# Three one-hot comparisons of 1,024 values in place of one of 3,072 in the bucket stage of a graph layer kernel

## The reference

```
gate = sigmoid(log u - log(1-u) + log_alpha)           # log_alpha from both ends' features
mask = clip(gate * (ZETA - GAMMA) + GAMMA, 0, 1)        # one weight per edge
d    = clip((segment_sum(mask, row) + EPS_DEG) ** -0.5, 0, 10)
out  = segment_sum(mask * d[row] * d[col] * x[col], row)
```

## Time and profile before

| | |
|---|---|
| median of three runs | 6101.76 us |
| profiled execution | 6092.52 us |
| its span | 6090.7 us |
| VectorE busy | 5120.7 us, 84% |
| TensorE matmuls busy | 4148.6 us, 68% |
| ScalarE busy | 2501.2 us, 41% |
| GpSimd busy | 1389.0 us, 23% |
| bucket stage of layer 0, first DMA issue to last one-hot | 3338.7 to 3867.5 us |
| bucket stage of layer 1, the same | 5548.4 to 6082.0 us |

### The profile page before, as it was taken

The page is one execution under the profiler, slowest core; times in us unless marked ns, Lnnn a source line. Parts: engine busy times, 40 slices in busy tenths (PEclk is TensorE's granted clock), DMA queues, the critical chain, the costliest instruction groups (busy, mean ns, idle before and its releaser), DMA issues. The chain is left out here.

```text
span 6090.7 us, 161651 instructions
## 1 busy us (share of the span) xinstructions
PE 4148.6 (68%) x56330; PEld 3706.6 (61%) x56330; DVE 5120.7 (84%) x10244; ACT 2501.2 (41%) x5126; POOL 1389.0 (23%) x1562
## 2 busy tenths in 40 slices
PE   3777777776597888835554666888888355554666
PEld 2666666665456888825443666558888344444565
DVE  8999999999446999989998777229999799997776
ACT  2666656564134555425554000245555155551000
POOL 0000000000002333300000888303333100004887
PEclk9777777776555555566776999755555577777999
DMA  3000000000136777569997898336767499997888
GB/s 71 0 0 0 0 0 0 0 0 1 14 12 215 232 233 232 192 218 331 329 330 280 298 310 299 113 101 231 234 230 232 143 317 330 330 330 267 310 313 282
DMA packets 428686, 1120.74 MB, mean 184 GB/s; under 512 B 206962, under 2 KB 212707, under 8 KB 428023
## 3 DMA queue, kind: packets, MB, share of 16 engines
q1 hardware_dynamic: 316700, 549.97, 29.3%
q0 software_dynamic: 65856, 316.89, 15.1%
q10 hardware_dynamic: 46036, 252.74, 10.9%
HBM read 873.65 MB, written 279.36 MB: 189 GB/s over the span
## 5 line engine op out<-in xcount | busy, mean ns | idle before, releaser
L1610 PE MATMUL psG<-y_window,area 128*128 128x64 bf16 x14976 | 675.1, 218 | 774.4 <-DVE area L1256 620.4
L1610 PEld LDWEIGHTS psG<-y_window,area 128*128 128x128 bf16 x14976 | 631.3, 115 | 818.4 <-issue 504.5
L586 POOL DMA_INDIRECT work<-msg_d,widx x396 | 584.0, 1475 | 1643.4 <-issue 1605.7
L642 ACT ACTIVATE work<-iota,work 128x149 bf16<-128x149 f32 x2496 | 789.0, 406 | 0.0
L1429 PE MATMUL psG<-area,work 128*128 128x112 bf16 x2496 | 550.8, 390 | 338.0 <-DVE area L978 338.0
L1622 PE MATMUL psG<-work,edge 128*128 128x192 bf16 x4752 | 483.2, 263 | 306.9 <-DVE edge L1290 306.9
L1622 PEld LDWEIGHTS psG<-work,edge 128*128 128x128 bf16 x4752 | 448.0, 147 | 341.5 <-DVE edge L1290 259.9
L1429 PEld LDWEIGHTS psG<-area,work 128*128 128x128 bf16 x2496 | 357.4, 148 | 486.3 <-issue 341.3
L1422 PE MATMUL psG<-work,merge 128*128 128x148 bf16 x4992 | 546.3, 294 | 68.2 <-ACT work L642 68.2
L1422 PEld LDWEIGHTS psG<-work,merge 128*128 128x128 bf16 x4992 | 529.6, 132 | 90.9 <-issue 66.6
L816 ACT ACTIVATE work<-merge 128x1024 bf16<-128x1024 f32 x312 | 330.1, 1058 | 549.4 <-DVE merge L1266 549.4
(11 more groups left out here) (268 smaller groups left out, 8385.7 us busy)
## 6 DMA issues: line engine op xcount, KB each, us to landing
msg_d<-work ACTq DMA_DIRECT2D x312, 776.0 KB, 4.6
area<-rlo_d SPq DMA_DIRECT2D x312, 512.0 KB, 4.4
merge<-crel_d SPq DMA_DIRECT2D x312, 512.0 KB, 5.0
area<-crelp_d SPq DMA_DIRECT2D x312, 512.0 KB, 5.7
y_window<-y_d SPq DMA_DIRECT2D x312, 48.0 KB, 3.6
y_d<-cur SPq DMA_DIRECT2D x7, 1008.0 KB, 3.8
y_d<-work SPq DMA_DIRECT2D x7, 1008.0 KB, 4.8
work<-msg_d,widx POOLq DMA_INDIRECT x396, 6.2
```

Source lines behind the costliest of these rows:

```text
L586: pool.indirect_dma_start(out=windows[par][:, rows.start:rows.stop, :].rearrange("p s w -> p (s w)"), out_offset=None, in_=msg_d, in_offse ...
L642: ins = act.activation(below[:, h, k, :], iota_all[:, :], ACT.Sign, bias=keyf[:, bass.ds(t * CT + k, 1)], scale=-1.0)
L1610: ins = pe.matmul(psG[:, 2 * h + k // CH, k % CH * D:(k % CH + 1) * D], col_one_hots[:, h, k * P:(k + 1) * P], y_window[:, h, m * D:(m + 1 ...
```

## The change

The one-hots of a bucket are made group by group. Each of the three comparisons writes 1,024 values per partition (8 rows by 128 nodes) and counts `q_hots_ready` by one, so that a bucket counts three. TensorE waits before its matmuls 0, 8 and 16 for the count of the group that they use, and no longer for all three groups before the first. The count of matmuls, their order, the DMAs, the buffers and the values stay as they are.

```
-                    dve.tensor_tensor(q_one_hots[s], iota_rows.unsqueeze(1).to_broadcast([P, WG, P, WIN]),
-                                      ids[:, s, :].rearrange("p (g s) -> p g s", g=WG).unsqueeze(2).to_broadcast([P, WG, P, WIN]), ALU.is_equal).then_inc(q_hots_ready, 1)
+                    for g in range(WG):
+                        dve.tensor_tensor(q_one_hots[s][:, g, :, :], iota_rows,
+                                          ids[:, s, g * WIN:(g + 1) * WIN].unsqueeze(1).to_broadcast([P, P, WIN]), ALU.is_equal).then_inc(q_hots_ready, 1)
...
-                        pe.wait_ge(q_hots_ready, n + 1)
                         for r in range(WG * WIN):
+                            if r % WIN == 0:
+                                pe.wait_ge(q_hots_ready, n * WG + r // WIN + 1)
                             ins = pe.matmul(psG[:, slot_, 0:MW], q_one_hots[slot_][:, r // WIN, :, r % WIN], windows[slot_][:, r, 0:MW],
                                             start=r == 0, stop=r == WG * WIN - 1)
```

## The result

The changed kernel took 5891.02 us (median of four runs, 5883.25 to 5891.75) against 6100.96 us for the kernel before (median of four): a ratio of 0.9652, 95% interval 0.9637 to 0.9668. The profiled execution took 5890.85 us, 201.7 us less than the one before; its span is 5889.1 us. The forecast was 5985 us with a range down to 5925: the sign and the mechanism were right, but little more than half of the gain was forecast. The time is that of the rival with VectorE as the bound at 2.9 us a bucket, and half of its reason holds as well, as the experiments show.

The account below looks back on a forecast made before the run. GpSimd's DMA issuing, held by VectorE's comparisons, was taken to bound the bucket stages at 3.585 us a bucket; transfers at 3.2 would follow, saving 113 us over 294 buckets plus 2 us: 5985 us, range 5925 to 6065.

Parts of the forecast that it names:

- the rival with VectorE as the bound at 2.9 us a bucket: Bucket stages: transfers are no bound, VectorE sets 2.9 us a bucket; 5899 us, chance 0.12.
- The stage is paced by GpSimd's issuing: Bucket stages before the change: two GpSimd DMA issues with gaps take 3.56 us a bucket, matching the measured pace.
- An issue that starts while a comparison runs stands still until its end and then needs 0.87 us: GpSimd's DMA issues in the bucket stages: held by VectorE's comparison, losing 0.48 us an issue, 282 us over 294 buckets.
- Does the lock open between two comparisons?: Step claiming, from the mask stage, that GpSimd gets in between back-to-back comparisons, so thirds hold an issue only one third.
- The slower rival: Bucket stages: issues are not let in between thirds, each bucket loses 0.15 us; 6146 us, chance 0.06.
- Part 1: VectorE's added fixed cost per bucket: three comparisons take 1.91 us against 1.76, +0.15 us, ends 0 and 0.30.
- Part 2: VectorE's floor per bucket with data there: 2.67 us before, 2.82 with thirds, 2.9 with small gaps.
- Part 3: GpSimd's issuing per bucket after the change: two issues of 1.10 us with 0.30 us gaps, 2.8 us.
- Part 4: Transfers become the longest: 3.07 us a bucket at 349 GB/s, 3.25 at 330, 3.2 taken.
- The sum: (3.585 - 3.2) x 294 = 113 us plus 2 us at the ends, 115 us off 6092.5; median forecast 5985 us.
- Part 5: TensorE starts 1.07 us earlier, worth nothing inside the bucket stage, 2 us over the last buckets of both layers.
- GpSimd waits more than 0.3 us for TensorE would say it has run ahead: Sign in the bucket stage: GpSimd has reached the buffers' limit and the transfers are the bound.

Follow-up runs that it names:

- e5: The kernel before with every indirect DMA fetching half its rows, as many issues; 6088.76 us, ratio 0.9986.
- e9: The kernel before, one comparison of 3,072 values, with `ids` in float32 in PSUM, so one comparison input in SBUF; 6312.37 us.
- e10: The kernel before, one comparison of 3,072 values, with `ids` in float32 in SBUF, so both comparison inputs in SBUF; 6537.95 us.
- e4: The changed kernel with every indirect DMA fetching half its rows, as many issues; 5882.83 us.
- e8: The kernel before, making only 128 of a bucket's 3,072 one-hot values, which all matmuls use; 5890.78 us.
- e1: The changed kernel, still three comparisons, but TensorE waits for all three before its first matmul; 5894.16 us.
- e3: The changed kernel with only the first group's comparison made, its one-hots used by all 24 matmuls; 5891.75 us.
- e7: The changed kernel with the previous bucket's sum moved behind the first third and its scaling behind the second; 5890.24 us.

## Why the prediction was right or wrong

- "The stage is paced by GpSimd's issuing": right. e5 shows it from the other side: half the bytes, the same 3.57 us.
- "An issue that starts while a comparison runs stands still until its end and then needs 0.87 us": right. In the kernel before 290 of the 302 issues that started within a comparison ended 0.85 to 0.90 us after its end; the other 12 started in its first 0.04 us and took 1.00 us. e9 with e10 give the cause.
- "Does the lock open between two comparisons?": it does. In the changed kernel's timeline an issue ends 0.87 us after the first third, while the second and the third run. The slower rival falls with it. The Trainium skill (SBUF — State Buffer, Who interferes with whom) infers that `tensor_tensor` spares descriptor generation, since that needs the write interface alone. For an indirect DMA, whose offsets lie in SBUF, the runs show otherwise: 3.96 us in e10 against 0.99 us in e9. The same section's rule on two SBUF inputs agrees with both.
- Part 1, +0.15 us for thirds: the row of three is 1.90 us in the timeline against 1.91. Right.
- Part 2, VectorE's floor of 2.82 to 2.9 us: 2.84 in e4 and in the changed kernel, layer 0. Right.
- Part 3, issues of 1.10 us and 2.8 us a bucket: (210.9 + 117.5) / 294 = 1.117 us, 2.84 us, and none over 1.51 us. Right.
- **Part 4 is the step that failed**: "At 349 a bucket takes 3.07 us, at 330 3.25. I take 3.2". The sum's term for the transfers was mis-sized: their limit is 380 GB/s and 2.81 us a bucket in layer 0 (e8), not 3.2. I read a limit from the best 10 us and from a stage of another kind of transfer. Even those 10 us were short of work: their DMA share is 0.95, where e8 at its limit has 1.00. The trace had said so at a finer grain: the DMA view of 20 us of the kernel before, in 40 slices of 0.5 us (first row the share in tenths), has slices of over 400 GB/s beside others at a quarter of it.

```profile
DMA  9994296899951967999659379895969999999995
GB/s 410 410 354 180 106 199 161 310 385 422 397 199 75 137 87 273 385 447 410 242 213 174 99 273 410 348 248 149 236 248 410 422 422 422 342 422 422 422 404 211
```

  The longest run of full slices there is at 404 to 422 but for one of 342, 410 in the mean, above what the queue holds over a stage (380), so these overstate as the 10 us windows understate; the truth lay between. With the measured 2.89 us in place of 3.2 the sum gives (3.585 - 2.89) x 294 + 2 = 206 us, and the profiled executions differ by 202. With the transfers at 2.81 us, VectorE's 2.82 to 2.9 us of part 2 becomes the longest term in layer 0. (The sum's own last step gives 5986.5 and is written as 5985; nothing hangs on it.)
- Part 5, TensorE's early start worth 2 us: e1 puts it at 3 to 9 us. Small, as forecast; the runs do not tell it more finely.
- The rival "the transfers are no bound at all and VectorE is" has the measured time and half of the cause. VectorE does set the pace in layer 0, and the sign listed for it, VectorE without idle time at 2.9 us, was seen: 0.6 us of waits for data in 332 us. But the transfers are a bound right behind it: in e3 VectorE had 1.0 us less to do and the time stayed, and in e7 the shorter cycle turned into waits for data. That the two limits lie so close is chance of this kernel. The rival should have had more than 0.12, since nothing in the rows excluded rates above 349.
- "GpSimd waits more than 0.3 us for TensorE would say it has run ahead": seen in layer 1, where the waits for buffers reach 1.4 us (`POOL area L586 <- PE psG L1624: 8.3, 17, 1.4` in the table of waits). Layer 1 is 0.07 us a bucket slower than layer 0. In e8, with neither VectorE nor the issues in the way, it is as well (2.85 and 2.92 us a bucket between the first and the last `ids`), so the difference lies with the transfers or with what else they share. The output stored during that stage is a candidate that I did not try; it has the size: from 5480 to 5850 us the changed kernel's DMA view counts 137.39 MB of indirect transfers and 4.10 MB in another queue, which leaves the indirect ones 371 GB/s against 379 in layer 0, 2% or 0.06 us a bucket.

## What to carry to other kernels

When one engine's instruction holds another's, count how many of the held ones fit between two of the holders, and not the mean delay: here one comparison of 1.76 us let through one issue where a bucket needs two, and cutting it in two or three removed 196 or 210 us for 0.07 us of VectorE's time a cut. Cut no further than that, as the eight pieces show. And when a bound is taken away, do not read the next resource's limit from the stage in which it was starved; look at the finest slices, which bound it from above, and keep that end in the range.

## What the runs showed of the hardware

- A VectorE `tensor_tensor` with both inputs in SBUF holds an indirect DMA issue from GpSimd until 0.87 us after its end, for comparisons of 0.69, 1.76 and 3.36 us alike. With one input in PSUM it doesn't (0.99 us). The length of the record is not always the length of the hold: e8's comparison of 128 values has a record of 0.72 us, but the next VectorE instruction starts 0.34 us after it, and an issue at 3344.88 us, 0.43 us into such a record, took 1.00 us. No delay of VectorE by GpSimd in return is seen: the thirds took 676 to 752 ns, median 685.
- The held instruction gets in between two comparisons although the second one starts 0.08 us before the first one ends (three of 0.69 us take 1.90 us).
- Indirect transfers from HBM that fetch 6.2 and 3.1 KB for each partition reached 380 GB/s (e8, over 332 us), against 300 GB/s in the same stage before.
- TensorE's granted clock in the bucket stage of layer 0 was in the mean 0.93 of its upper level (2.4 GHz) before and 0.99 after, with TensorE busy for 355 of 523 us and 330 of 420 us. No run tested what the clock is worth here; that it is little is argued from TensorE not being the bound in either.
